# A graph layer on one core: tiles ranked one by one, 49 tiles in 13 blocks without padding

## The reference

```
gnn = relu(segment_sum(xw[src, type] * weight, dst))     # xw = xn @ W_type, 32 types from 8 bases
mix = xn + LN(relu([xn, LN(msg @ Wm)] @ W1) @ W2)         # msg: linear attention over all nodes, 8 heads
x   = x + gnn + mix
f   = sum over 8 experts of w_e * Wo_e(relu(bn(W2_e relu(bn(W1_e LN(x))))))   # w = softmax of a mean
out = x + f
```

## Time and profile before

| | us |
|---|---|
| three timed runs, median | 3714.89 |
| the profiled execution, its own time | 3694.45 |
| its span, first to last instruction | 3692.7 |
| TensorE busy | 3076.4 (83%) |
| VectorE busy | 2330.3 (63%) |
| GpSimd busy | 2075.6 (56%) |
| ScalarE busy | 1013.5 (27%) |
| end of the last step (last line 1340) | 3477.8 |
| first matmul of block 12's experts | 3607.5 |

### The profile page before, as it was taken

One profiled execution on the slowest core, in us unless ns is written; L12 is line 12 of the kernel. 1 busy time (PEld: TensorE's weight loads), 2 busy tenths in 40 slices (PEclk: granted clock), 3 DMA queues, 4 the chain that ended last, 5 costly groups with the idle time before them and its releaser, 6 DMA issues.

```text
span 3692.7 us, 64865 instructions
## 1 busy us (share of the span) xinstructions
PE 3076.4 (83%) x18282; PEld 2683.8 (73%) x18282; DVE 2330.3 (63%) x6228; ACT 1013.5 (27%) x1678; POOL 2075.6 (56%) x2825
## 2 busy tenths in 40 slices
PE   0068888555778999899998999999899998989889
PEld 0047777555667888788887888878788887878777
DVE  4746665555556776677667666666667666767523
ACT  0022232100112323233323223333333332333344
POOL 0056566666656666666666666666666666666300
PEclk9999999777888999999999999999999999999999
DMA  7369898766768878787778878787787878778633
GB/s 197 114 207 294 272 295 274 198 194 190 218 199 255 265 253 254 233 265 250 252 248 256 256 235 257 244 252 250 247 256 241 269 236 259 246 252 261 203 115 111
DMA packets 647443, 864.86 MB, mean 234 GB/s; under 512 B 63831, under 2 KB 524197, under 8 KB 646816
## 3 DMA queue, kind: packets, MB, share of 16 engines
q1 hardware_dynamic: 511092, 550.00, 46.0%
q0 software_dynamic: 95776, 262.27, 24.4%
q10 hardware_dynamic: 40140, 47.81, 3.9%
HBM read 552.23 MB, written 316.84 MB: 235 GB/s over the span
## 4 chain that ended last, share of the span: by engine, by line
PE 58%; issue 16%; DVE 8%; DMA 7%; POOL 5%; another core or an unknown queue 2%; SPq 2%; ACT 1%; POOLq 0%; DVEq 0%; ACTq 0%
PE PS L1775 56%; DMA steps<-normed_nodes,steps 6%; POOL steps L775 5%; DVE steps L1374 2%; DVE h_low L1063 1%; DVE steps L1256 1%; PE PS L1845 1%; SPq L425 1%; DVE feed L1063 1%; DMA mixbuf<-in_x_dram 1%; DVE steps L1331 1%; SPq L370 0%; POOL hold L773 0%; DVE feed L1690 0%
## 5 line engine op out<-in xcount | busy, mean ns | idle before, releaser
L775 POOL DMA_INDIRECT steps<-normed_nodes,steps x1968 | 1957.9, 995 | 1133.2 <-issue 507.2
L1374 DVE SCALAR_TENSOR_TENSOR steps<-steps,PS 128x256 f32<-128x256 f32 x1968 | 943.2, 479 | 916.1 <-PE PS L1775 522.4
L1775 PE MATMUL PS<-steps 128*128 128x128 f32 x7872 | 1197.3, 290 | 290.6 <-issue 164.8
L1775 PEld LDWEIGHTS PS<-steps 128*128 128x128 f32 x7872 | 1100.3, 202 | 395.4 <-issue 275.5
L1775 PE MATMUL PS<-bases_s,feed 128*128 128x256 f32 x1664 | 393.8, 381 | 2.3 <-issue 2.3
L964 ACT ACTIVATE feed<-PS,bnc 128x512 f32<-128x512 f32 x416 | 317.8, 776 | 162.6 <-PE PS L1775 131.3
L1775 PEld LDWEIGHTS PS<-bases_s,feed 128*128 128x128 f32 x1664 | 305.9, 191 | 40.4 <-issue 3.0
L1331 DVE TENSOR_TENSOR steps<-steps 128x512 f32<-128x512 f32 x495 | 330.0, 688 | 4.2
L1775 PE MATMUL PS<-w_one,feed 128*128 128x256 f32 (+1 forms) x1028 | 306.6, 432 | 1.6 <-issue 1.6
L963 ACT ACTIVATE h_high<-PS,bnc 128x512 fp32r<-128x512 f32 x208 | 161.9, 778 | 517.0 <-PE PS L1775 357.5
L971 ACT COPY feed<-feed 128x1024 f32<-128x1024 f32 x104 | 217.7, 2093 | 195.1 <-DMA feed<-step_sums 131.9
(11 more groups left out here) (215 smaller groups left out, 3116.1 us busy)
## 6 DMA issues: line engine op xcount, KB each, us to landing
step_sums<-steps SPq DMA_DIRECT2D x492, 512.0 KB
split_in<-expert_split SPq DMA_DIRECT2D x104, 1024.0 KB
feed<-step_sums SPq DMA_DIRECT2D x416, 128.0 KB
steps<-step_types SPq DMA_DIRECT2D x126, 256.0 KB
steps<-normed_nodes,steps POOLq DMA_INDIRECT x1968
mixbuf<-mix_hidden SPq DMA_DIRECT2D x53, 256.0 KB
w_zero<-in_L_ffn_Wo_dram SPq DMA_DIRECT2D x52, 256.0 KB
w_one<-in_L_ffn_Wo_dram SPq DMA_DIRECT2D x52, 256.0 KB
```

Of the source, the lines that this page charges most:

```text
L775: pool.indirect_dma_start(out=ring[:, k, :], out_offset=None, in_=xnD, in_offset=bass.IndirectOffsetOnAxis(ap=idxc[:, u, k:k + 1], axis=0) ...
L1374: dve.scalar_tensor_tensor(acc[:, k % ACCR, :], acc[:, (k - 1) % ACCR, :], keepc[:, k:k + 1], PS[:, a:a + C], ALU.mult, ALU.add).then_inc( ...
L1775: return pe.matmul(o, a, b, start=start, stop=stop)
```

## The change

The change ranks single tiles. A block is the next 3 or 4 tiles of the ranking: 3, ten times 4, 3, 3, together 49. There is no padding tile. The number of steps and iterations stays 1968 and 123, and blocks still begin at iteration 27 and take 8 iterations. The first block's mixing takes 6 iterations and not 8, and `PLAIN` is 4.

- **Sizes.** Every loop over a block's tiles, and the width of every tile that holds a block (512 columns for 4 tiles), now goes by `SIZES[b]`: blocks 0, 11 and 12 have 3 tiles and 384 columns. In block 11 nothing is combined at i = 5; in block 10 and 11 nothing is mixed in the last two iterations.
- **Ranking.** 48 bounds and 49 tiles stand where 12 and 13 stood. The rank of a tile is found with a tile on each partition, and one more matmul spreads ranks and places to all partitions. The comparison tables of 16 slots are 784 elements wide, before 208.
- **Store.** Each of a block's tiles gets its own pair of DMAs (128 KB, or tile 48's 106 KB), each pair after two register loads.
- **SyncE.** It loads up to 9 tile numbers a block. Blocks 2 to 9 stay a hardware loop; the others are written out. The last sums of a block's second tile are read after a further wait, for the stores of the block's first iteration. Four stores of zeros to padding rows at the start are gone.

```diff
 SUP = 4
-SUPERS = -(-TILES // SUP)
-PADTILES = SUP * SUPERS
+SIZES = (3,) + 10 * (4,) + (3, 3)
+BLOCKS = len(SIZES)
+AT = tuple(sum(SIZES[:b]) for b in range(BLOCKS + 1))
-PLAIN = 2
+PLAIN = 4
 M2_AT = M1_ITS + PLAIN
-FIRST = M2_AT + 2 * SUP
-ITERS = FIRST + (SUPERS - 1) * BLK
+FIRST = M2_AT + 2 * SIZES[0]
+ITERS = FIRST + (BLOCKS - 1) * BLK
...
-            for t, a, b in ((queryD, 0, C), (shiftD, 0, C), (hiddenD, 0, C), (hiddenD, C, 2 * C)):
-                sp.dma_start(rows(t[TILES * P:PADTILES * P, a:b], PADTILES - TILES),
-                             zero.to_broadcast([P, PADTILES - TILES, C])).then_inc(sem("setup_out"), 16)
...
-                        load_agg(b, 0, s[2])
-                    if prep and i in COMB[:-1] and k == 7:
-                        load_agg(b, COMB.index(i) + 1, s[2])
+                        load_agg(b, 0, tiles[0])
+                    if prep and i in COMB[:size(b) - 1] and k == 7:
+                        if i == COMB[0] and it0 is not None:
+                            kept(it0 + 1)
+                        load_agg(b, COMB.index(i) + 1, tiles[COMB.index(i) + 1])
...
+                w = SIZES[fed] * P
-                        act.activation(h1_high[:, k, :], bank(b0 + k), ACT.Relu, bias=bias, scale=scale)
+                        act.activation(h1_high[:, k, 0:w], bank(b0 + k, 0, w), ACT.Relu, bias=bias, scale=scale)
...
             def store(fed):
-                act.load(oregs[0:1], order[0:1, 0, bass.ds(fed, 1)])
-                act.load(oregs[1:2], order[0:1, 1, bass.ds(fed, 1)])
-                wait_apart(act, "o_upd", LEAD + SUP * (EXPERTS + 1) * (fed + 1))
-                act.dma_start(out[bass.ds(full * (SUP * P), SUP * P), :].rearrange("(j p) n -> p j n", p=P),
-                              oacc[:, :, :], cond=(s < SUPERS - 1)).then_inc(sem("out_st"), 16)
-                act.dma_start(out[(TILES - 1) * P:NODES, :], oacc[0:LAST, 0, :], cond=(s > SUPERS - 2)
-                              ).then_inc(sem("out_st"), 16)
+                for j in range(SIZES[fed]):
+                    act.load(oregs[0:1], order[0:1, 0, AT[fed] + j:AT[fed] + j + 1])
+                    act.load(oregs[1:2], order[0:1, 1, AT[fed] + j:AT[fed] + j + 1])
+                    tile = act.snap(oregs[0], min_val=0, max_val=TILES - 1)
+                    full = act.snap(oregs[1], min_val=0, max_val=TILES - 2)
+                    if j == 0:
+                        wait_apart(act, "o_upd", LEAD + (EXPERTS + 1) * AT[fed + 1])
+                    act.dma_start(out[bass.ds(full * P, P), :], oacc[:, j, :], cond=(tile < TILES - 1)
+                                  ).then_inc(sem("out_st"), 16)
+                    act.dma_start(out[(TILES - 1) * P:NODES, :], oacc[0:LAST, j, :], cond=(tile > TILES - 2)
+                                  ).then_inc(sem("out_st"), 16)
...
-            link(tt(less, every(s_ord[:, :], SUPERS), each(s_ord[:, :], SUPERS), ALU.is_lt))
-            link(dve.tensor_reduce(s_rk[:, :], less, AX.X, ALU.add))
+            link(tt(s_own, s_ord, ident[:, 0:TILES], ALU.mult))
+            link(dve.tensor_reduce(ord_col[:, :], s_own, AX.X, ALU.add))
+            link(dve.tensor_scalar(s_less, s_ord, ord_col[:, 0:1], None, ALU.is_lt))
+            link(dve.tensor_reduce(rk_col[:, :], s_less, AX.X, ALU.add))
...
-            link(tt(cmp_a[:, :, :], each(slot_no[:, :], SUPERS), every(s_new[:, :], SB), ALU.is_ge))
+            link(tt(cmp_a[:, :, :], each(slot_no[:, :], TILES), every(s_new, SB), ALU.is_ge))
...
-                for j in range(SUP):
+                for j in range(SIZES[b]):
...
-            def layer(o, w, frm, low, low_name, low_count, b0=B_L):
+            def layer(o, n, w, frm, low, low_name, low_count, b0=B_L):
-                    return mm(bank(b0 + o), left[:, h, o * P:(o + 1) * P], right[:, h, :], start, stop)
+                    return mm(bank(b0 + o, 0, n * P), left[:, h, o * P:(o + 1) * P], right[:, h, 0:n * P], start, stop)
```

More of the change, by code:

```diff
@@ L37, with size, at @@
 SUP = 4
-SUPERS = -(-TILES // SUP)
-PADTILES = SUP * SUPERS
-SGROUPS = SUP * P // GN
-DUMP = SUPERS * SGROUPS
+SIZES = (3,) + 10 * (4,) + (3, 3)
+BLOCKS = len(SIZES)
+AT = tuple(sum(SIZES[:b]) for b in range(BLOCKS + 1))
+assert AT[BLOCKS] == TILES and max(SIZES) == SUP
+TGROUPS = P // GN
+DUMP = TILES * TGROUPS
+def size(b):
+    return SIZES[b] if isinstance(b, int) else SUP
+def at(b):
+    return AT[b] if isinstance(b, int) else SUP * b - 1
+assert all(AT[b] == SUP * b - 1 and SIZES[b] == SUP for b in range(1, BLOCKS - 2))
 UN = 16
@@ L72 @@
 assert (M1_ITS - 1) * M1_PER + 1 == TILES and M1_ITS - 1 == 2 * EXPERTS
-assert all((FIRST + BLK * b) * UN >= -(-STEPS * (b + 1) // SUPERS) for b in range(SUPERS))
+KEPT = (0, 1, 1, 1)
+assert all(min(FIRST + BLK * b + KEPT[j], ITERS) * UN >= STEPS * (AT[b] + j + 1) // TILES
+           for b in range(BLOCKS) for j in range(SIZES[b]))
 CALM_END, LIGHT_END = 16, 36
@@ L615, in mix_it, with block_its @@
                         load_hidden(n + 1, nxt)
-            def block_its(it0, b, s, fed, prep):
-                for at in range(SPAN):
-                    i, k = divmod(at, UN)
-                    j, m = divmod(at, MIX_AT)
+            def block_its(it0, b, tiles, fed, prep):
+                for step in range(SPAN):
+                    i, k = divmod(step, UN)
+                    j, m = divmod(step, MIX_AT)
                     if it0 is not None:
@@ L684, in _ @@
                         next_types(it)
-            for n in range(SUP):
-                first, second = supers(0)
+            for n in range(SIZES[0]):
+                tile, nxt = tiles_from(n, 2)
                 if n == 1:
@@ L1006, in block_its @@
+            def block_its(b, fed, prep):
+                for step in range(SPAN):
+                    i, k = divmod(step, UN)
+                    j, m = divmod(step, MIX_AT)
+                    n = AT[b + 1] + j
+                    mixed = b + 1 < BLOCKS and j < SIZES[b + 1]
                     if fed is not None:
                         for e in range(EXPERTS):
-                            if at == EXP_AT * e + 1:
+                            if step == EXP_AT * e + 1:
                                 hidden(fed, e, 0)
-                            if at == EXP_AT * e + 10:
+                            if step == EXP_AT * e + 10:
@@ L1241, in _ @@
+            dve.wait_ge(sem("count_sum"), 3)
+            seq, new = (bank(2, 2 * P + n * TILES, 2 * P + (n + 1) * TILES) for n in range(2))
+            link(dve.tensor_copy(s_new, new))
+            link(tt(s_off, s_at[:, 0:TILES], s_new, ALU.subtract))
+            link(tt(s_end, s_new, s_len, ALU.add))
             link(dve.memset(order[:, :, :], 0))
[L1242 to L1243 removed]
@@ L1719, in block_its @@
                         pair(it0 + i, p)
-                    if fed is not None and at == 0:
+                    if fed is not None and half == 0:
                         router_take(fed)
-                    if prep and i in COMB and p == 6:
+                    if prep and i in COMB[:SIZES[b]] and p == 6:
                         sum_up(b, COMB.index(i), fed)
@@ L1727, in block_its @@
                         behind(it0 + i, p)
-                    if fed is not None and at == 2:
+                    if fed is not None and half == 2:
                         o_begin(fed)
                     if mixed:
-                        mixing(n, m, MIX, True, j, fed is not None or j > 0)
+                        mixing(n, m, MIX, True)
                     elif prep and j == 0:
@@ L2130, in _ @@
                 else:
-                    for n in range(SUP):
+                    for n in range(SIZES[fed]):
                         third(fed, e - 1, n)
```

404 lines of the change are left out of this document (203 added, 201 removed).

## The result

The kernel before has a median of 3714.95 us over four (3710.57 to 3716.34), the changed kernel 3671.35 us over four (3668.58 to 3680.44). The ratio is 0.9891, with a 95% interval of 0.9874 to 0.9908: 1.1% faster. The forecast was 3667, its range 3642 to 3692.

The account below looks back on a forecast made before the run. GpSimd's gathers were taken to pace the blocks, with TensorE near its limit; behind the last step a tile less has full price. Terms sum to -47.8 us from 3694.45, giving 3646.6, and with the 20.4 offset 3667; range 3642 to 3692.

Parts of the forecast that it names:

- The width: Behind the last step: a matmul of 384 columns takes 0.180 us instead of 0.233, so 0.053 saved each.
- The stretch with block 12's preparation: Behind the last step, block 11's experts and block 12's preparation: 25.7 us less, bounds 14 and 30.
- The store: ScalarE's DMAs and register loads: T = 1.0 us a tile; +6.9 us at three ends, bounds 4.5 and 11.8.
- cover: At ten mid-kernel block ends a late ScalarE costs 0, since gathers go on and TensorE catches up with them.
- The last block: Block 12's experts: 19.2 us less, bounds 10 and 21, before the store's term at the block's start and end.
- The rival of a dear store: Register loads make ScalarE late at every block's end and TensorE waits; slower, 3744 us at T = 2.5; chance 0.05.
- SyncE's new wait: SyncE waits for the stores of the block's first iteration; with its register loads costed at 0, upper end 1 us a block.
- The blocks: Blocks 1 to 11: gathers set the pace, sum within 10 us of 2323; TensorE's saved work brings next to nothing.
- The 5 us counted for block 1: Of 34 us that TensorE loses in blocks 1, 10 and 11, 5 count, nearly all in block 1, where the ring is full.
- Iterations 15 to 34: Ahead of and around block 0: 3.2 us less from two iterations without mixing, 2 less from a dropped combine.
- The start: DMA issues gone, 2.5 us less; VectorE's wider operations, counting and small operations, 4.8 more; net +2.3, bounds -2 and +6.
- The offset of 20.4 us: Profiled execution of the kernel before stood 20.4 us below its runs' median; the same was added to the forecast.

Follow-up runs that it names:

- width512: Changed kernel with the first and second layers' matmuls of its last two fed blocks 512 columns wide again: 3689.25 us, ratio 0.9954 to the kernel before.
- store_regs: Changed kernel with each store's register loads gathered into two loads of 4 or 3 registers, ahead of the store's wait: 3664.48 us, ratio 0.9894 to the kernel before.
- act_delay: Changed kernel with 24 tiny chained copies on ScalarE ahead of the store at block ends 0 to 9: 3680.89 us, ratio 0.9899 to the kernel before.
- no_low_mid: Changed kernel without the matmuls on the inputs' low halves in the blocks that feed 2 to 9: 3669.74 us, ratio 0.9902 to the kernel before.
- pool_hold: Changed kernel with one more small write and wait on GpSimd in each iteration from 36 on: 3710.99 us, ratio 0.9980 to the kernel before.
- last_two: Changed kernel with gathered register loads and blocks of 3, eleven times 4, and 2 tiles: 3667.27 us, ratio 0.9905 to the kernel before.

## Why the prediction was right, and where it was not

The means by stage, in us, from two profiles of the kernel before and three of the changed one, against the prediction's sum. "T" is the prediction's letter for ScalarE's time per stored tile.

| stretch | before | after | measured | forecast |
| --- | --- | --- | --- | --- |
| start to iteration 14 | 638.0 | 638.9 | +1.0 | +2.3 |
| iterations 15 to 34 | 519.0 | 522.9 | +3.8 | -5.2 |
| blocks 1 to 11 | 2323.5 | 2325.8 | +2.3 | -6.9 |
| from the last step to block 12's experts | 131.2 | 109.3 | -21.9 | -23.1 |
| last block | 84.0 | 72.8 | -11.2 | -14.9 |
| sum | | | -25.9 | -47.8 |

**The width** was right: 0.177 us for 0.180, cycle 6.83 for 6.9, and `width512` takes it away alone. The spacing at 512 columns stayed 0.233. The Trainium skill, "TensorE: Matmul & The Clock Gate", section "Back-to-back issue gap", states a sustained spacing of about 131 ns at 512 columns and 81 at 128, from which 114 at 384 is an estimate; here it is 233 and 177 ns, and the measurement decides.

**The stretch with block 12's preparation** was right in its parts: 15.66 us with a combine for 15.8 forecast, 9.82 without, so a combine costs 5.84 (5.9). Without the store's term it lost 27.4 us, for 25.7. The prediction's "76 us more" for block 12's experts is a slip: from 3607.5 us to the end of the span it is 85. No term uses it.

**The store** failed as a term: "two register loads per tile, which no row shows". The rows are there in the trace of before (0.29 and 0.28 us). With them T is 0.74 + 0.26 + 0.57 = 1.57. In the changed kernel the first load of a pair has a median of 0.47 instead, which is 0.18 more; the last 0.18 of the pitch I can't place. Measured is 1.93, outside my ends of 0.74 and 1.55. In the three ends behind the steps it delayed by 5.5 + 3.9 + 3.9 = 13.2 us, for 6.9. `store_regs` takes the loads away and gives 7 us back. The prediction's working for mid-kernel has two slips beside: 3.7 us is the mean of ten gaps and not of eleven, and without cover 10 x (4T - 3.7) is 3 us at T = 1 and 25 at 1.55, not 5 and 21. The Trainium skill, "Runtime: NRT & Kernel Launch", section "Instruction fetch mechanics", has about 200 ns for a register loaded from HBM; here a load of one from SBUF has a median of 280 or 470 ns.

**The last block** lost 3.7 us less than the sum had. Six full cycles brought 13.3 us (6 x 2.14 = 12.8 forecast) and the end 1.0 (1.5). It is the first expert that failed: it should have become 0.5 us shorter and became 3.1 longer. 1.6 us of that are the dearer store. For the other 2.0 the sum had no term. The lower granted clock behind TensorE's longer wait (0.50, for 0.74 and 0.57 before) lies there and works that way; no run takes it away alone.

**The rival of a dear store** had its break-even at T = 1.9, and T was 1.93. It still did not happen, since its larger part, the payment at ten ends in mid-kernel, has cover: 4 us later at each, and no 40 us in the blocks. 3 us less at each end (`store_regs`) and 3 us more (`act_delay`) change little. The cost near 0 was right. SyncE's new wait I also had at 0; no run takes it away.

**The blocks.** Their sum stayed within 10 us of 2323; block 2 had 212.2, 223.5 and 215.7 (206 to 219 said). That TensorE's saved work brings nothing over many blocks is shown by `no_low_mid`. The prediction's reason is only half right. It read from the earlier trace rows that GpSimd stood still for other reasons than its own for 1% of the time; then nearly all of 60 us put into it would have arrived, and 24 did (`pool_hold`). Those rows could not tell this: ahead of 235 of the 1021 gathers the wait that ended last was for a matmul of TensorE. The 5 us counted for block 1 did come: it takes 196.4, 194.9 and 195.0 us for 199.7 and 199.2. By the end of block 3 they are gone again (blocks 1 to 3 together 622 to 626 us, before 622 and 624). And blocks 3 to 10 take 1702.2, 1700.1 and 1706.0 us for 1695.0 and 1694.0, 8 us more, for which the sum has nothing. `store_regs` has 1701.5 there, which speaks against the stores; SyncE's new wait stands in `last_two` too, with 1694.3. The cause is open.

**Iterations 15 to 34** failed: -5.2 forecast, +3.8 measured, of which executions differ by 7 to 10. I took a plain iteration to be 1.6 us shorter than one with mixing from one pair of stretches. Plain ones are shorter in every profile, 21.9 and 22.7 us before and 22.4 to 22.8 after. But those with mixing became longer, 24.3 and 24.9 before and 24.9 to 26.1 after, so that iterations 17 to 26 together have 240.2 and 243.3 before, and 246.6, 240.6 and 242.9 after. The length of one kind depends on the others. The gain is at most small, and its sign is open.

**The start** was right: in the first pair of profiles VectorE's counting and ranking has +4.9 (4.8 forecast) and what lies ahead of it -2.6 (-2.5), net +2.3 at 144 us. At the start of iteration 0 it is still +2.6: 231.0 to 232.1 us in the three profiles, for 228.8 and 229.2. Behind that it is lost in differences between executions: the stage's mean is +1.0, and kernels whose edits all lie behind iteration 14 have 638 to 649 us.

**The number.** Against the profiles the sum was 22 us too large: 9 in iterations 15 to 34, 9 in the blocks, and 5 behind the last step, less 1 at the start. Against the medians it was 4 us too large in the first comparison (47.9 for 43.6), and 7 to 16 by the ratios of all three (0.9891, 0.9915 and 0.9912, so 31 to 41 us). Most of what lies between profiles and medians is chance again: the two profiled executions of the kernel before stood 20 and 4 us below the medians of their series, those of the changed kernel within 3 of theirs. The offset of 20.4 us was such an accident. So that 3667 lies within 5 us of 3671 is in part luck; the terms behind the last step carried it, and the terms ahead of it can't be seen.

## What to carry to other kernels

Behind the last step of this pipelined loop a tile, a matmul or a store has nearly its full price; inside it, work taken from an engine that is 93% busy may bring nothing, and a late engine may cost nothing. Look every small operation up by the tile that it reads before you write that no row shows it. Before a forecast is tied to a median through one profiled execution, ask by how much stages differ between executions.

## What the runs showed of the hardware

- A load of one register from SBUF takes ScalarE 0.28 or 0.47 us in the median, a load of four 0.92; a pair of loads per tile nearly doubled the pitch of the stores, from 1.02 to 1.93 us.
- Unconditional DMAs of 64 rows, issued on ScalarE, stood 0.65 us apart in the median and 0.8 in the mean, about as much as a whole conditional pair of a tile, of which one moves no data (0.71).
- Behind an idle stretch of 5.97 us TensorE's granted clock was 0.50 for the next 6.9 us; behind one of 2.21 us it was 0.74 and 0.57 in two executions.
- One more write and wait of 0.93 us an iteration on GpSimd, which was busy for 64% of the stretch, made it 0.37 us longer.
